# Single-core graph kernel: segment-sum passes with positions loaded one by one, and with ScalarE making some one-hots of the first pass

## The reference, cut to what matters

```python
def sage_conv(x, edge_index, W_l, b_l, W_r, num_segments):
    src, dst = (edge_index[0], edge_index[1])
    agg = jax.ops.segment_sum(x[src], dst, num_segments=num_segments)
    return agg @ W_l.T + b_l + x @ W_r.T
h = jax.nn.relu(sage_conv(x, edge_index, W_l_in, b_l_in, W_r_in, n))
out = sage_conv(h, edge_index, W_l_out, b_l_out, W_r_out, n)
x = _layernorm(x + out)
# then an attention layer over the same edges (segment_max, exp, segment_sum), and a second layernorm
```

## Time and profile before

| what | us |
|---|---|
| median of three executions | 3997.3 |
| the profiled execution, its own time | 4001.15 |
| its span, first to last instruction | 3999.3 |
| busy in the span: PE, DVE, ACT, POOL | 2838.4, 2714.7, 2490.8, 2638.2 |
| pass `sum_x`, about | 75 to 935 |
| pass `sum_y`, about | 985 to 1720 |

### The profile page before, as it was taken

The page is one execution under the profiler, slowest core; times in us unless marked ns, Lnnn a source line. Parts: engine busy times, 40 slices in busy tenths (PEclk is TensorE's granted clock), DMA queues, the critical chain, the costliest instruction groups (busy, mean ns, idle before and its releaser), DMA issues. The chain is left out here.

```text
span 3999.3 us, 82215 instructions
## 1 busy us (share of the span) xinstructions
PE 2838.4 (71%) x28125; PEld 2379.6 (60%) x28125; DVE 2714.7 (68%) x7548; ACT 2490.8 (62%) x7102; POOL 2638.2 (66%) x2669
## 2 busy tenths in 40 slices
PE   3688788887888888874567666676666666667646
PEld 2566566664777777764456655565555665656644
DVE  7898766774455455562467777777876777777776
ACT  4566666775666566630167766787666776677745
POOL 3466765774655565427777777777777777777735
PEclk9999989998999999985567776677776777677767
DMA  3677875113666676723333333333333333333311
GB/s 88 237 284 312 315 313 213 21 20 118 223 232 234 222 237 222 237 92 69 76 77 87 90 85 76 87 94 86 85 82 78 93 87 83 79 82 88 89 31 39
DMA packets 285952, 536.14 MB, mean 134 GB/s; under 512 B 116631, under 2 KB 203217, under 8 KB 278902
## 3 DMA queue, kind: packets, MB, share of 16 engines
q1 hardware_dynamic: 200032, 452.07, 32.7%
q0 software_dynamic: 80256, 76.21, 10.2%
q10 hardware_dynamic: 5246, 2.56, 0.2%
HBM read 355.50 MB, written 175.09 MB: 133 GB/s over the span
## 5 line engine op out<-in xcount | busy, mean ns | idle before, releaser
L2034 POOL DMA_INDIRECT scratch<-fs_scratch,src_idx x728 | 728.8, 1001 | 222.0 <-issue 221.4
L892 POOL DMA_INDIRECT gath<-x_parts,src_idx x532 | 538.8, 1013 | 316.6 <-issue 191.5
L949 ACT ACTIVATE scratch<-sum_x_ps_c 128x600 int32<-128x600 f32 (+5 forms) x690 | 520.0, 770 | 311.2 <-PE sum_x_ps_c L981 266.6
L1066 DVE TENSOR_SCALAR e_tab<-scratch,e_tab 128x700 bf16<-128x700 f16 (+8 forms) x1380 | 526.1, 423 | 257.8 <-PE sum_y_ps_c L981 226.5
L892 POOL DMA_INDIRECT gath<-y_parts,src_idx x412 | 406.6, 987 | 291.6 <-issue 121.0
L2162 ACT ACTIVATE scratch<-scratch,bias,weight 128x32 f32<-128x32 f32 x1360 | 483.7, 399 | 77.2 <-DVE bias L2232 77.2
L2076 PEld LDWEIGHTS ps_e<-fdw,scratch 128*128 128x128 f32 x3136 | 494.3, 239 | 23.2
L2243 DVE SCALAR_TENSOR_TENSOR scratch<-ps_e,attn_sb 128x128 f32<-128x128 f32 x784 | 189.4, 284 | 429.0 <-PE ps_e L2076 427.8
L2076 PE MATMUL ps_e<-fdw,scratch 128*128 128x66 f32 x3136 | 478.0, 319 | 0.0
L949 ACT ACTIVATE scratch<-sum_y_ps_c 128x700 int32<-128x700 f32 (+2 forms) x348 | 280.1, 832 | 279.7 <-PE sum_y_ps_c L981 274.5
L1006 PEld LDWEIGHTS sum_x_ps_d<-parts,scratch 128*128 128x128 f16 x7400 | 383.3, 101 | 102.3 <-ACT scratch L949 44.4
(11 more groups left out here) (363 smaller groups left out, 6241.3 us busy)
## 6 DMA issues: line engine op xcount, KB each, us to landing
count_scratch<-scratch SPq DMA_DIRECT2D x48, 3200.0 KB
scratch<-count_scratch SPq DMA_DIRECT2D x192, 800.0 KB
onehot<-rel_scratch SPq DMA_DIRECT2D x196, 256.0 KB
scratch<-in_edge_attr_2x SPq DMA_DIRECT2D x390, 128.0 KB
fdw<-fd_scratch SPq DMA_DIRECT2D x392, 33.0 KB
scratch<-fs_scratch,src_idx POOLq DMA_INDIRECT x728
gath<-x_parts,src_idx POOLq DMA_INDIRECT x532
gath<-y_parts,src_idx POOLq DMA_INDIRECT x412
```

The lines of the kernel that those rows point to most:

```text
L892: pool.indirect_dma_start(out=rows_in(s, t), out_offset=None, in_=table_dram, in_offset=bass.IndirectOffsetOnAxis(ap=src_idx[:, g, k:k + 1 ...
L949: act.activation(to, ps_c[u % pairs][:, :, 0:q].rearrange("p h (d a) -> p h a d", d=d), ACT.Copy).then_inc(kept, 1)
L1066: d = dve.tensor_scalar(cells[:, n % RING, i * width:(i + 1) * width], count_up[:, 0:width], head_key[:, tile:tile + 1], head_weight[:, ti ...
L2034: pool.indirect_dma_start(out=rows_of(m)[:, t, :], out_offset=None, in_=fs_dram, in_offset=bass.IndirectOffsetOnAxis(ap=src_idx[:, g, k:k ...
```

## The change

`lent` becomes half the slots in `sum_x` (33 of 67), so that ScalarE makes the one-hots of slots 0 to 32 there and VectorE those of slots 33 to 66. `sum_y` stays as it was in this. And in both passes each slot loads its own two positions by two loads of one word, where every fourth slot loaded eight words by one load.

```diff
-            lent, pairs = slots if read else 0, 2
+            lent, pairs = slots if read else slots // 2, 2
...
-                    made, starts, heads_added, tails_added = plan.first_item, [], 0, 0
+                    made, heads_added, tails_added = plan.first_item, 0, 0
...
                         for i in adds.get(step, ()):
-                            if i % SLOTS == 0:
-                                last = min(G, (n0 + i + SLOTS) * SG)
-                                starts = nc.values_load_multi_w_load_instructions(
-                                    win[0:1, (n0 + i) * SG:last], engines=DVE_ENGINE, min_val=0, max_val=N,
-                                    skip_runtime_bounds_check_because=CLAMPED)[1]
+                            at = (n0 + i) * SG
+                            starts = [nc.values_load_multi_w_load_instructions(
+                                win[0:1, at + g:at + g + 1], engines=DVE_ENGINE, min_val=0, max_val=N,
+                                skip_runtime_bounds_check_because=CLAMPED)[1][0] for g in range(SG)]
                             dve.wait_ge(summed, i + 1)
...
-                                    to = table_a[rows, bass.ds(starts[i % SLOTS * SG + g], WINDOW)]
+                                    to = table_a[rows, bass.ds(starts[g], WINDOW)]
```

## The result

| | median us | lowest to highest | executions |
|---|---|---|---|
| before | 3990.7 | 3984.5 to 4000.4 | 8 |
| changed | 4009.7 | 4005.5 to 4023.9 | 8 |

The ratio of changed to before is 1.0048, with a 95% interval of 1.0032 to 1.0064: 19 us slower, where 15 us faster was forecast. It lies inside the stated range and near rival B (4015 us). A second comparison, on another chip together with the last experiments, gave 1.0037 (1.0024 to 1.0049), 14 us slower.

What follows compares the result with a forecast made beforehand. VectorE was taken to set the pace in `sum_x`'s first stretch (138 to 544 us). Terms -1 - 1 - 17 + 2 = -17 us, rounded to -15, took the 3997.3 us median to 3982 us, range 3955 to 4015.

Steps and rivals of the forecast that it cites:

- rival B: First stretch of `sum_x`: ScalarE becomes the bound, TensorE meets each one-hot at its free pace, stall 2.9 us; 4015 us, chance 0.15.
- second half of `sum_x`: From 544 us on: fewer cell waits and a better clock, less 6 us of new short waits; -17 us.
- cell waits, first stretch: `sum_x`, 138 to 544 us: 51 of TensorE's 58.4 us of waits for cells from VectorE go.
- waits for L1092, first stretch: `sum_x`, 138 to 544 us: 9 of TensorE's 12.0 us of waits for VectorE's L1092 go.
- waits for copies, first stretch: `sum_x`, 138 to 544 us: TensorE's waits for ScalarE add 63 us over 33 slots, less 4 us that overlap.
- clock, first stretch: `sum_x`, 138 to 544 us: granted clock left at 0.93, as in `sum_y` with lent one-hots; no time added.
- start: Start of `sum_x`, where VectorE's one-hot L1040 stands ahead of the first cells: -1 us.
- `sum_y`: Eight one-word loads for one eight-word load per four slots, beside a half-idle VectorE: +2 us (0 to +8).
- the stall of 1.9 us a slot: First stretch of `sum_x`: PSUM buffer free at 5.5 us behind a lent one-hot, wanted by TensorE at 3.6 us; 33 slots, +63 us.
- the 4 us of overlap: First stretch of `sum_x`: about 4 of the present 14 us of waits for ScalarE coincide with the new stalls.
- Rival D: One-word loads cost 0.6 to 1.05 us each under the stores of counts, so splitting gains nothing; 4007 us, chance 0.12.
- The estimate of 0.2 us for the steps behind a load: VectorE's queue: register and semaphore steps add some 0.2 us to each slot's load cost of up to 0.6 us without cover.

Runs made afterwards that it cites:

- e1_lent: The kernel before with only the one-hots of slots 0 to 32 of `sum_x` lent to ScalarE, eight-word loads kept: 4050.5 us, ratio 1.0135 to before.
- e2_shorter: The changed kernel without the last instruction of each lent one-hot block in `sum_x`, so its sums are wrong: 3966.7 us, ratio 0.9938 to the kernel before.
- e1_loads: The changed kernel with no one-hots lent in `sum_x`, so only the one-word loads remain: 3947.7 us, ratio 0.9889 to the kernel before.

## Why the prediction was wrong, point by point

The terms of the sum, each against the traces:

| term | predicted | measured |
|---|---|---|
| second half of `sum_x` | -17 | -17 (391 to 374 us) |
| cell waits, first stretch | -51 | -49 (58.4 to 9.6) |
| waits for L1092, first stretch | -9 | -11 (12.0 to 1.3) |
| waits for copies, first stretch | +59 (63 less 4) | **+81** (14.5 to 95.9) |
| clock, first stretch | 0 | **+12** (busy 322.3 to 334.0, same matmuls) |
| start | -1 | -4 |
| `sum_y` | +2 | +1 and +6 in the two traces, inside the spread |
| sum | -17 | +13 with the +1; the medians say +19 and +14 |

Right: what bounded each stretch, what a block costs ScalarE (3.52 predicted, 3.53 measured), that it is the next unit's copy that queues, and the terms of the loads and of VectorE, within a few us. Of the signs that the prediction named, these came true: waits for cells under 15 us, no gap over 2 us before the add (1.8 at most), a clock of 0.97 from 577 to 706 us. The waits for copies, 95.9 us, lie between its 60 to 80 and rival B's 100. `sum_x` ends 16 us later instead of 15 earlier. The first stretch moved by 37 us, over the 25 that it named as wrong at its root.

**The step that failed is the stall of 1.9 us a slot, and with it the 4 us of overlap.** The trace of the changed kernel lets me redo the step block by block. For each block I take the count whose copy stands in front of it and go to the start of the third count after it, the first that needs a buffer from behind the block. In that time TensorE works, or waits for ScalarE, or waits for something else (means in us, 31 blocks):

| blocks that start at | blocks | count to third count | own work | waits for ScalarE |
|---|---|---|---|---|
| 133 to 233 us | 7 | 5.3 | 2.7 | 2.0 |
| 233 to 354 us | 9 | 6.2 | 3.2 | 2.9 |
| 354 to 458 us | 7 | 6.4 | 3.7 | 2.8 |
| 458 to 577 us | 8 | 7.2 | 5.0 | 2.2 |
| all | 31 | 6.3 | 3.65 | **2.5** |
| predicted | 33 | 5.5 | 3.6 | 1.9 |

So TensorE's pace was right: 3.65 us of its own work for three units, 1.2 us a unit. What was too small is the time until the buffer is free. The block begins 1.5 us after the count, not 1.2. The next copy starts 0.08 us behind it and takes 0.87, not 0.8, and TensorE starts another 0.14 us later, or more where its own work came last. The prediction took a count of 300 columns, but the later blocks stand mostly among units of 400 and 500. At the block of 281 us ScalarE's L958 stands behind the block too, and TensorE waits 5.04 us:

```profile
284.99 1.15 ACT L958 ACTIVATE table_a<-sum_x_ps_s,b_out 32x512 f32<-32x512 f32 x1
...
287.06 0.83 PE L981 MATMUL sum_x_ps_c<-e_tab,onehot 128*128 128x400 bf16 x2 [5.04 <-ACT scratch L949]
```

That happens at 2 of the 31 blocks. In all TensorE waits 77 us for ScalarE at these third counts, where 63 were put. The other waits for copies were to fall by 4 us and rose by some 4, from 14.5 to 19. These two make the 22 us between +59 and +81.

The gain of the loads did not make this loss. `e1_lent`, with the long loads, shows the same own work, 3.64 us for three units, and 2.2 us of waiting for ScalarE at a block. The neighbour that I checked the 1.9 us against, the same figure a block in `sum_y`, has units 735/348 = 2.1 us apart; it agreed with a wrong number for another reason.

**The second failure is the clock left at zero.** I took 0.93 from `sum_y`. The same matmuls took 12 us more at 0.90, and `e2_shorter` shows it the other way round.

Rival B, with a chance of 0.15, came nearest: 18 us over the kernel before forecast, 19 and 14 measured. That is luck in part. It has TensorE at its free pace of 0.87 us between the blocks and a stall of 2.9 us, and the traces show 1.2 us and 2.5. It puts the threshold of a clear loss at 2.7 us, which was not reached. Its waits for copies came 11 us too high (92 against 81) and its clock 12 us too low, and the two cancel.

**The loads** were right in their effect. Over all 238 the median is 0.310 us and the longest 1.06, as forecast. But that median hides two kinds, 0.918 us beside the stores of counts and 0.303 to 0.308 elsewhere. The row it was taken from the earlier trace rows has loads of `head_win`, which stand mostly between two stores: the trace of the changed kernel has 46 of them up to 700 us, and at 41 the queue of the stores is less than a fifth busy; these take 0.305 us, none over 0.32. At 85 of the 86 loads of `win` there it is busier. Rival D's condition, 0.6 to 1.05 us a load under the stores, was thus fulfilled, though not the sign it was given (a median over 0.6) and not its price: two loads of 0.9 us stay under the cover of two units, as the 1.9 us of `e1_loads`' longest wait shows. The estimate of 0.2 us for the steps behind a load had no row; where VectorE idles before an add, 0.24 us lie between the load's end and the add (median, 40 gaps in the changed kernel's trace). And the gain of the loads, had they come alone, was sized too low: `e1_loads` won 26 us in the first stretch too (409 to 383).

## What to carry to other kernels

Before moving work to an engine with idle time, look at what stands behind it in that engine's order and how many buffers its partner has. The stall is the time until the next buffer is free, less the work that the partner has meanwhile. Take both from the units among which the blocks fall, and not the first from a small unit and the second from the mean: here that made 1.9 us of 2.5. Then add what stops of that length cost in clock, by a stretch that has them. If work must be moved, cut it in pieces behind different units, which took 53 us off here. And look first at why a long wait is long: here the eight-word load, from one badly placed first word, was worth 50 us and more, while no way of lending gained anything that shows.

## What the runs showed of the hardware

- A load of registers from `win` takes 0.30 us for one word, 0.54 for two and 0.61 for eight that begin at a multiple of eight, but 1.85 us for eight that begin two words past one. An even first word is not enough, since 258 is even; whether a multiple of four would do was not tried.
- The Trainium skill, Runtime: NRT & Kernel Launch, Instruction fetch mechanics, gives about 200 ns a register even in bulk, for loads that the page describes as coming from HBM. `win` lies in SBUF. The eight from a wrong word are near that figure (0.23 us a word), the aligned eight, 0.076 us a word, are far below it.
- Beside the stores of counts the same loads take three times as long: 0.92, 1.76, 1.82 and 6.0 us. They don't in `sum_y` (0.308 us for one word), where the counts are read back and all DMA moves 225 GB/s. What the loads contend for beside the stores was not tested.
- Stops of TensorE of 3 to 4 us were followed by counts of 0.71 us in place of 0.42. The clock in the first stretch was 0.88 where one-hots and long loads both stopped it, 0.90 and 0.91 with the one-hots in blocks, 0.92 with the long loads, and 0.93 to 0.97 in the kernels with neither full blocks nor the long loads.
